# Attention scores in plain fp32 on four 32-row groups of the array, with the negated row maximum as a 17th feature

## The reference, cut to what matters

```python
def _attn(q, k, v, causal):
    s = jnp.einsum('blhd,bmhd->bhlm', q, k)
    if causal:
        s = jnp.where(mask, s, -jnp.inf)
    p = jax.nn.softmax(s, axis=-1)
    return jnp.einsum('bhlm,bmhd->blhd', p, v)
```

## Time and profile before

| what | value |
|---|---|
| median of 3 runs | 5721.84 us (5720.23 to 5731.34) |
| profiled execution, span first to last instruction | 5720.3 us; no other own time is given for it |
| mean granted TensorE clock | 0.920 |
| TensorE matmul busy | 4624.6 us (81%), 34992 matmuls |
| VectorE, ScalarE, GpSimd busy | 3590.9 (63%), 2441.3 (43%), 1298.8 us (23%) |
| chain that ended last | PE 48%, DVE 25%, issue 16%, POOL 6%, ACT 3% |

### The profile page before, as it was taken

How to read it: one execution, slowest core, us unless ns; L and a number is a source line. 1 busy time by engine, 2 the same in 40 slices (tenths; PEclk the granted TensorE clock), 3 DMA queues, 4 the chain that set the end, 5 groups by cost and what they waited for, 6 DMA issues and landing times.

```text
span 5720.3 us, 99465 instructions
## 1 busy us (share of the span) xinstructions
PE 4624.6 (81%) x34992; PEld 3728.5 (65%) x34992; DVE 3590.9 (63%) x7863; ACT 2441.3 (43%) x5121; POOL 1298.8 (23%) x1924
## 2 busy tenths in 40 slices
PE   4888888888888888888888888888888888888886
PEld 3666666666666666666666666666666666666665
DVE  4666666666666666666666666666666666666663
ACT  1444444444444444444444444444444444444442
POOL 0222222222222222222222222222222222222221
PEclk7899999999999999999999999999999999999997
DMA  1000000000000000000000000000000000000000
GB/s 55 9 10 10 9 12 10 10 10 12 9 10 12 10 10 10 11 10 10 10 12 9 10 12 10 10 12 10 10 10 12 10 9 11 11 10 10 12 6 5
DMA packets 64812, 63.61 MB, mean 11 GB/s; under 512 B 9648, under 2 KB 64048, under 8 KB 64304
## 3 DMA queue, kind: packets, MB, share of 16 engines
q1 hardware_dynamic: 64304, 56.61, 3.2%
HBM read 39.81 MB, written 16.78 MB: 10 GB/s over the span
## 4 chain that ended last, share of the span: by engine, by line
PE 48%; DVE 25%; issue 16%; POOL 6%; ACT 3%; DVEq 0%; POOLq 0%; ACTq 0%
PE sc L470 10%; DVE nm_c L757 5%; PE B L335 4%; PE A L340 3%; PE A L342 3%; PE A L341 3%; POOL hid_hi L1076 3%; PE C L340 3%; PE C L342 3%; PE C L341 3%; PE B L340 2%; PE A L481 2%; PE sc L465 2%; PE B L481 2%; DVE at_lo L626 2%
## 5 line engine op out<-in xcount | busy, mean ns | idle before, releaser
L947 ACT ACTIVATE pt<-sc 128x512 f32<-128x512 f32 x1024 | 564.1, 599 | 415.0 <-PE sc L470 402.8
L1046 POOL TENSOR_TENSOR rstd<-bmv,eps_t 128x1 f32<-128x1 f32 x384 | 72.7, 189 | 1894.9 <-DVE bmv L674 1894.9
L626 DVE TENSOR_TENSOR hid_lo<-hid,hid_hi 128x512 fp32r<-128x512 f32 x256 | 264.7, 1070 | 353.2 <-POOL hid_hi L1076 353.2
L921 ACT CAST qt<-B 32x512 fp32r<-32x512 f32 x512 | 295.7, 577 | 183.9 <-PE B L335 179.4
L1076 POOL TENSOR_TENSOR hid_hi<-hid,ones_f 128x512 fp32r<-128x512 f32 x256 | 264.7, 1054 | 453.4 <-ACT hid L977 452.7
L757 DVE TENSOR_REDUCE nm_s<-sc 128x4 fp32r<-128x512 f32 x512 | 338.8, 682 | 12.4 <-PE sc L442 5.7
L335 PE MATMUL B<-ident,att 128*128 128x128 f32 x512 | 114.9, 308 | 279.3 <-DVE att L771 279.3
L757 DVE TENSOR_REDUCE nm_c<-sc 128x4 fp32r<-128x512 f32 x512 | 316.2, 674 | 0.0
L340 PE MATMUL C<-w_f_hi,hid_hi 128*128 128x256 f32 x1024 | 302.4, 295 | 3.6 <-POOL hid_hi L1076 3.0
L678 DVE TENSOR_SCALAR xhat<-x,bmv,rstd 128x256 f32<-128x256 f32 x256 | 207.0, 808 | 144.3 <-POOL rstd L1048 144.3
L921 ACT CAST qt<-A 32x512 fp32r<-32x512 f32 x512 | 294.9, 576 | 4.7 <-PE A L335 0.3
(11 more groups left out here) (249 smaller groups left out, 14323.5 us busy)
## 6 DMA issues: line engine op xcount, KB each, us to landing
rows_in<-in_x SPq DMA_DIRECT2D x128, 128.0 KB, 2.0
rows_in<-in_ctx SPq DMA_DIRECT2D x128, 128.0 KB, 2.1
out<-o_out SPq DMA_DIRECT2D x128, 128.0 KB, 1.7
pt<-in_L_xattn_fc_w SPq DMA_DIRECT2D x1, 1024.0 KB, 4.8
rows_in<-in_L_xattn_fc_w SPq DMA_DIRECT2D x1, 1024.0 KB, 6.8
pt<-in_L_xattn_sa_wq SPq DMA_DIRECT2D x1, 256.0 KB, 8.6
rows_in<-in_L_xattn_sa_wk SPq DMA_DIRECT2D x1, 256.0 KB, 8.6
pt<-in_L_xattn_sa_wv SPq DMA_DIRECT2D x1, 256.0 KB, 2.7
```

The source lines that it names most:

```text
L626: dve.tensor_tensor(out, a, hi.bitcast(F32), ALU.subtract).then_inc(signal, 1)
L921: w = act.copy(qt[c][part, :, b, :], bank_of[c]["q"][part, :].rearrange("p (g q) -> p g q", q=P))
L947: act.activation(pt[c][:, g, :, :].rearrange("p b q -> p (b q)"), sc[:, g, :], ACT.Exp)\
```

## The change

Keys and queries are no longer split or doubled. The rotary step writes each head's 16 features into a 32-wide slot of a padded tile (`qkz`, `qcz`, `kcz`): feature 17 of the keys is 1, feature 17 of the queries is where `maxima` writes the negated maximum, the rest is zero. Four transposes bring heads 4g+r to partitions 32r of group g. `scores` and `scores_t` are 16 plain fp32 matmuls each, 128 x 128 outputs, on array rows 32r to 32r+15 (or +31), r innermost, bank r of `sc` for row group r, with one semaphore step after the sixteenth. In place of `trm`, the queries with their maxima are transposed again (`trqm`) and copied once more (`qtm_`). `maxima` are two reductions of two banks each. Heads now lie in `sc`, `pt` and `osb` by (r, g), and `normalise` puts them back.

```diff
-                kh = keys_of(c, at)[0]
...
-                    for b in range(G):
-                        mm = pe.matmul(sc[:, g, b * P:(b + 1) * P], qt[c][:, g, b, :], kh[:, g, :],
-                                       start=(b == 0 and c == "c"), stop=(b == G - 1), skip_group_check=True)
-                    mm.then_inc(sc_[c]["sc"], 1)
+                    for r in range(G):
+                        rows = slice(32 * r, 32 * r + HD)
+                        mm = pe.matmul(sc[:, r, g * P:(g + 1) * P], qt[c][rows, g, :], kt[c][rows, g, :],
+                                       start=(g == 0 and c == "c"), stop=(g == G - 1), skip_group_check=True)
+                mm.then_inc(sc_[c]["sc"], 1)
...
-                pe.transpose(bank_of[c]["m"][:, 0:P], nm[c][:, :, :].rearrange("p b g -> p (b g)").bitcast(F32),
-                             ident[:, :]).then_inc(sc_[c]["trm"], 1)
+                transposes(bank_of[c]["m"], qz[c].rearrange("p h e -> p (h e)"), G).then_inc(sc_[c]["trqm"], 1)
...
-                pe.wait_ge(sc_[c]["mdiag"], n(at))
+                pe.wait_ge(sc_[c]["qtm"], n(at))
                 for g in range(G):
-                    pe.matmul(sc[:, g, :], ones_r[32 * g:32 * g + 32, :],
-                              mdiag[c][32 * g:32 * g + 32, :, :].rearrange("p b q -> p (b q)"), start=(c == "c"),
-                              stop=False, skip_group_check=True)
-                for g in range(G):
-                    for kk in (kh, kl):
-                        mm = pe.matmul(sc[:, g, :], kk[:, g, :], qt[c][:, g, :, :].rearrange("p b q -> p (b q)"),
-                                       start=False, stop=(kk is kl), skip_group_check=True)
-                    mm.then_inc(sc_[c]["sct"], 1)
+                    for r in range(G):
+                        rows = slice(32 * r, 32 * r + 32)
+                        mm = pe.matmul(sc[:, r, g * P:(g + 1) * P], kt[c][rows, g, :], qt[c][rows, g, :],
+                                       start=(g == 0 and c == "c"), stop=(g == G - 1), skip_group_check=True)
+                mm.then_inc(sc_[c]["sct"], 1)
...
-            def maxima(c, at, groups):
-                for g in groups:
-                    dve.wait_ge(sc_[c]["sc"], G * n(at, 0) + g + 1)
-                    dve.tensor_reduce(nm[c][:, g, 0:G], sc[:, g, :].rearrange("p (b k) -> p b k", b=G),
+            def maxima(c, at, halves):
+                dve.wait_ge(sc_[c]["sc"], n(at))
+                for h in halves:
+                    out = qz[c].rearrange("p (g r) e -> p r g e", r=G)[:, 2 * h:2 * h + 2, :, HD]
+                    dve.tensor_reduce(out, sc[:, 2 * h:2 * h + 2, :].rearrange("p r (g k) -> p r g k", g=G),
                                       AX_X, ALU.max, negate=True).then_inc(sc_[c]["nm"], 1)
...
                 act.wait_ge(sc_[c]["trq"], n(at))
...
-                for b in range(G):
-                    part = slice(32 * b, 32 * b + 32)
-                    w = act.copy(qt[c][part, :, b, :], bank_of[c]["q"][part, :].rearrange("p (g q) -> p g q", q=P))
-                w.then_inc(sc_[c]["qt"], 1)
...
+                need(act, sc_[c]["sct"], n(at, 0))
+                copy(qt[c][:, :, :], bank_of[c]["q"][:, :].rearrange("p (g q) -> p g q", q=P), sc_[c]["qt"])
+
+            def qtm_(c, at):
+                act.wait_ge(sc_[c]["trqm"], n(at))
+                copy(qt[c][:, :, :], bank_of[c]["m"][:, :].rearrange("p (g q) -> p g q", q=P), sc_[c]["qtm"])
...
+                act.wait_ge(sc_[c]["sct"], n(at))
                 for g in range(G):
-                    act.wait_ge(sc_[c]["sct"], G * n(at, 0) + g + 1)
                     act.activation(pt[c][:, g, :, :].rearrange("p b q -> p (b q)"), sc[:, g, :], ACT.Exp)\
                        .then_inc(sc_[c]["exp"], 1)
...
                 if X: residual("c", m, a if A else None)
+                if X: h3t_lo_(m)
                 if A: maxima("s", a, (1,) if X else (0, 1))
-                if X: h3t_lo_(m)
-                if A: maxima("s", a, (2, 3))
                 hid_lo_(i, u)
```

More of the change, by code:

```diff
@@ L95, in build @@
                 "c": [sb(f"vaug_c{i}", [P, H, 2 * HD]) for i in range(2)]}
[L96 to L99, removed]
+        kt = {c: sb(f"kt_{c}", [P, G, P]) for c in "sc"}
         tqk = sb("tqk", [P, 2 * E])
@@ L125, in build @@
         o_out = [sb(f"o_out{i}", [P, E]) for i in range(2)]
[L127 to L131, removed]
+        qt = {c: sb(f"qt_{c}", [P, G, P]) for c in "sc"}
         pt = dict.fromkeys("sc", sb("pt", [P, G, G, P]))
@@ L170, in build @@
         s = {n: sem("s_" + n) for n in names}
-        per_chain = ("qs_hi", "qs_lo", "trq", "qt", "sc", "nm", "trm", "mdiag", "sct", "exp", "pv", "osb", "tro",
+        per_chain = ("trq", "qt", "sc", "nm", "trqm", "qtm", "sct", "exp", "pv", "osb", "tro",
                      "rinv", "att", "tra", "at_hi", "at_lo", "y", "x", "xres")
@@ L396, in trq @@
             def trq(c, at):
-                pe.wait_ge(sc_[c]["qs_hi"], n(at))
-                pe.wait_ge(sc_[c]["qs_lo"], n(at))
+                pe.wait_ge(s["qkf" if c == "s" else "qcf"], n(at))
                 if c == "s":
@@ L409, in trk @@
                 need(pe, s["v_c"], n(at, 0))
-                transposes(A1, kd[:, :, :, :].rearrange("p h s e -> p (h s e)"), G).then_inc(s["trk"], 1)
+                transposes(A1, kz["s"].rearrange("p h e -> p (h e)"), G).then_inc(s["trk"], 1)
             def trkc(at):
-                pe.wait_ge(s["kcd"], n(at))
+                pe.wait_ge(s["kcf"], n(at))
                 pe.wait_ge(sc_["s"]["qt"], n(at, 2))
                 pe.wait_ge(s["cw"], n(at))
-                transposes(A0, kcd[:, :, :, :].rearrange("p h s e -> p (h s e)"), G).then_inc(s["trkc"], 1)
-            def keys_of(c, at):
-                return (skt_hi, skt_lo) if c == "s" else (kct_hi, kct_lo)
+                transposes(A0, kz["c"].rearrange("p h e -> p (h e)"), G).then_inc(s["trkc"], 1)
             def causal_mask(mask):
@@ L531, in f1 @@
                 need(pe, s["fpre"], n(f))
-                for q in ("kct_hi", "kct_lo", "tkc", "v_c"):
+                for q in ("kct", "tkc", "v_c"):
                     pe.wait_ge(s[q], n(k))
-                for q in ("skt_hi", "skt_lo"):
-                    pe.wait_ge(s[q], n(a))
+                pe.wait_ge(s["skt"], n(a))
                 for c in range(FC):
@@ L724, in rope @@
                 dve.wait_ge(sig_a, n(at))
-                dve.tensor_tensor(out[:, :], out[:, :], rsin[:, 0:width], ALU.add).then_inc(sig_o, 1)
+                for q in z_used:
+                    need(dve, q, n(at, 0))
+                dve.tensor_tensor(z[:, :, 0:HD], out[:, :].rearrange("p (h e) -> p h e", e=HD),
+                                  rsin[:, 0:width].rearrange("p (h e) -> p h e", e=HD), ALU.add).then_inc(sig_o, 1)
             def v_s(at):
```

148 lines of the change are left out of this document (54 added, 94 removed).

## The result

| | before | after |
|---|---|---|
| median | 5721.53 us (5720.23 to 5731.34, 4 runs) | 5822.96 us (5810.08 to 5826.21, 4 runs) |
| ratio to before, 95% | | 1.0167 [1.0151, 1.0182] |
| span of the profiled execution | 5720.3 us | 5820.9 us |
| mean granted TensorE clock | 0.920 | 0.884 |
| TensorE matmul busy | 4624.6 us | 4438.4 us |

A forecast was written before the change was run, and what follows sets the result against it. Bound by one tile's chain through the engines, except TensorE's full stretch from `qk` to `kvc`. Chain -0.7 plus clock +1.9 is +1.2 us for two tiles, times 64: 5722 + 77 = 5799 us; likeliest case 5735 to 5940, range 5630 to 5950.

The forecast's parts named there:

- The block: Each block of sixteen matmuls: 1.15 us taken, 2.0 at half clock, bounded between 1.10 and 3.8.
- The rule on modes: Before each block, changing tiling mode drains TensorE: at 0.22 us a change, a slot is 0.5 us worse than summed.
- Part 1: First scores of "s" and third layer norm: `xhat` waits for a reduction, +0.65 us a slot, +0.95 into F slots.
- Part 2: Cross scores to `scores_t c`: reductions end 0.43 us earlier, together -0.4 us a slot.
- Part 3: `scores_t c` to `fy`: 3.75 us at full clock against 5.06 before, -1.3 us; -0.45 with the block at half clock.
- Part 4: `scores_t s`, ahead of `trx2`: 0 in an F slot, -0.6 us in a mean N slot.
- Part 5: Granted clock: -1.4 us in the cross part, +0.8, +0.7, +1.4 and +0.4 around emptied stretches; +1.9 for two tiles.
- at nothing: Changes taken to cost or gain no time: fewer `qt_` copies, dropped splits and doublings, setup memsets, unchanged loop DMA.
- D: Rival: row groups take turns, each block 3.8 us instead of 1.15 in three places a slot; about 6750 us, chance 0.06.
- A: Rival, faster: clock doesn't fall in emptier stretches and rises in the cross part; 5590 to 5680 us, chance 0.24.
- B: Rival, a wash: clock losses of some 2 us cancel the gain, within 0.2% (11 us); chance 0.07.
- C: Rival: clock low nearly everywhere outside the full stretch, cross part too; up to 6190 us, put at 6050, chance 0.06.

The follow-up runs named there:

- Experiment 1: Changed kernel with the row group as outer loop in both blocks, so four matmuls in a row use the same 32 rows: 7153.68 us, ratio 1.2489.
- experiment 2: Changed kernel with the first reduction of "s" moved behind `xhat` of the third layer norm: 5680.51 us, ratio 0.9923 to the kernel before.
- experiment 3: Changed kernel with unread bf16 matmuls added in TensorE's waits (six behind `scores s`, three behind `trx`, four ahead of `trx2`): 5608.28 us, ratio 0.9789.
- experiment 10: Changed kernel, first reduction and second mask moved, unread matmuls added: 5462.34 us; kernel before, both masks moved, unread matmuls added: 5607.15 us.

## Why the prediction was right

The sign, the size and the mechanism held: 5799 us forecast, 5823 measured, inside the likeliest case.

- **The block.** 1.15 us taken, 1.17 measured; at half clock 2.0 taken, 2.09 seen (1.81 where the clock fell inside it). Experiment 1 shows the reason, that the order over row groups lets neighbours overlap, and what turns cost.
- **The rule on modes.** By it a slot would have been 0.5 us worse than my sum. In the cross part the copy of `qt_c` ends at 3063.02 + 0.59 = 3063.61 and the block's first record starts at 3063.65, so no drain is left to see where TensorE comes from a wait. Where full-height work stands just ahead, the mask starts at 3072.99 and the block at 3073.96: 0.97 later, as the sum had it (0.87 + 0.1). Before the change `tra s` began 0.87 behind such a mask and `scores` 0.69, so the block is 0.10 to 0.28 later than full-height work. Weight loads show more (`tra s` behind the mask that starts at 3038.79 before the change; the block behind the mask of 3072.99 after it):

```profile
3039.44 0.36 PEld L335 LDWEIGHTS B<-ident,att 128*128 128x128 f32 x2
```
```profile
3073.96 0.42 PEld L429 LDWEIGHTS sc<-kt_s,qt_s 16*128 16x128 f32 x12 [0.42 <-issue]
```

  The load of `tra s` begins 0.65 behind the start of its mask, that of the block 0.97 and not before the block itself: it isn't pulled ahead. What "TensorEngine Tiling (Array Packing)" in the Trainium skill, section Tiling Modes, says of a drain agrees with that; at 0.22 behind the mask's 0.87 the block would have begun 0.12 later than it did.
- **Part 1.** Reduction 1.21 taken, 1.22 measured; `xhat` 0.41 taken with POOL idle, 0.40 measured (first timeline after, 3076.34; 0.80 beside POOL's `x2b` in experiment 2); +0.65 a slot forecast, +0.60 measured and taken back by experiment 2.
- **Part 2.** -0.4 forecast; -0.51 + 0.10 and -0.51 + 0.07 measured.
- **Part 3.** The forecast mean was 0.8 x 3.75 + 0.2 x 4.6 = 3.9, against a mean before that I took from one slot at 5.06. Measured 4.29 in F slots and 3.94 in N slots, from 4.92 and 4.81: -0.63 and -0.87, where -1.13 was forecast. The length at full clock was right (3.75 taken, 3.77 measured), but -1.3 set it against a 5.06 that was mostly half clock: with the clock at full on both sides the gain is 4.28 - 3.77 = 0.51, and all else in this term was a bet on the clock. The stretch met half clock, wholly or in part, in 34 of 54 F slots and 13 of 54 N slots, where one in five was forecast.
- **Part 4.** N slot -1.03 against -0.6; F slot +0.31 against 0.
- **Part 5, the clock.** Into an F slot the terms of parts 1 and 5 together were 0.95 + 0.8 = 1.75; T to `y s` grew by 2.27. This term was too small by 0.5: the half clock reached `tra s` and `y s` too (first windows above). Into an N slot 0.65 + 0.7 = 1.35 were forecast and 0.32 measured: `f1` did run slower (294 to 344 ns for its first product), but the stretch as a whole got 0.28 shorter. I take it that most of the loss stayed hidden behind GELU's pipeline, which no run shows by itself. Ahead of `pv s` +1.4 and +0.4 were forecast, +1.12 and +0.60 measured. Some 0.5 us a pair that I had at nothing went to `pv s` to `scores c` (7.42 to 7.61 and 7.48 to 7.59) and to `fy` to `tro c` (+0.19 in F slots, +0.02 in N slots).
- **The sum.** +1.2 us a pair forecast, +1.7 measured by the slots. The term into the N slot was 1.0 us too dear; against it stood 0.5 too little into the F slot, 0.8 too much gain in part 3 and the 0.5 at nothing. That the sum came so near is in part luck; that its sign held is not, since experiment 3 takes 215 us off by the clock alone.
- **Rivals.** D: excluded by experiment 1. A needed a mean clock of 0.93 or more: it was 0.884. B, within 0.2%, is excluded by 1.0167 [1.0151, 1.0182]. C would have had half clock through the cross part: `scores c` took 1.17 us in each of the 108 slots, and `scores_t c` to `fy` was at full clock throughout in 61 of 108.

What stays open: how far each of the added groups behind `scores s` and behind `trx` acts alone, why the clock falls in the cross block in some slots and not in others, and what the change is worth against the kernel before with the clock at full in every stretch of both.

## What to carry to other kernels

In a kernel whose TensorE waits for a chain, matmul work that is taken away is worth only its part on the chain, and the stretch that it leaves empty can cost the granted clock of all that follows: price every emptied stretch by what runs next, at half clock. One semaphore step for a whole block of side-by-side matmuls moves every consumer behind the block, so ask what stood in the chain's waits before, and move it behind the chain's own instruction (here that alone turned +1.7% into -0.8%). A part of what a reordering gives may be clock and overlaps with the next one's; hold the clock in waits, with unread matmuls if there is nothing better, and then measure the moves again.

## What the runs showed of the hardware that I had not expected

- A full stretch did not bring the clock back. In experiment 1 TensorE was busy for 7.03 of 7.10 us, the last 5.10 of them in matmuls on one group of 32 rows after the other, and the granted clock stayed at 0.50 throughout (third and fourth window there); in the kernel before it was back at full after 6.47 of 6.90 us of mostly full-array matmuls. What makes the difference between the two was not tried.
- Added work made the kernel faster by 3.7% (experiment 3 against the changed kernel). Standing in a wait, it cost little where it cost anything: `y s` to `trx2` of N slots 4.45 us after 4.24 there, T to `trx3` 3.22 after 3.05 in experiment 10.
